# Layer 2's second feed-forward projection as 7 block products on one Trainium2 core

## The reference, cut to what matters

```
mod = silu(c) @ W_mod + b_mod
sh_msa, sc_msa, g_msa, sh_mlp, sc_mlp, g_mlp = split(mod, 6)        # one row of each per sequence
x = x + g_msa * attention(modulate(layernorm(x), sh_msa, sc_msa))
x = x + g_mlp * (gelu(modulate(layernorm(x), sh_mlp, sc_mlp) @ W1 + b1) @ W2 + b2)
```

## Time and profile before

| | |
|---|---|
| median of 3 runs | 2615.79 us (2615.1 to 2616.05) |
| the profiled execution | 2611.51 us, of which the span is 2609.7 us |
| PE busy | 2472.3 us, 95% of the span |
| DVE, ACT, POOL busy | 1777.8, 1208.8 and 546.5 us |
| layer 2's feed-forward part on PE | 1819.0 to 2040.8 us |
| layer 3's attention, then its feed-forward part | to about 2324 us, then to the end |

### The profile page before, as it was taken

One profiled execution on the slowest core, in us unless ns is written; L12 is line 12 of the kernel. 1 busy time (PEld: TensorE's weight loads), 2 busy tenths in 40 slices (PEclk: granted clock), 3 DMA queues, 4 the chain that ended last, 5 costly groups with the idle time before them and its releaser, 6 DMA issues.

```text
span 2609.7 us, 63484 instructions
## 1 busy us (share of the span) xinstructions
PE 2472.3 (95%) x25325; PEld 1913.4 (73%) x25325; DVE 1777.8 (68%) x3912; ACT 1208.8 (46%) x2525; POOL 546.5 (21%) x530
## 2 busy tenths in 40 slices
PE   7998999999999956999999999999999899889999
PEld 6886566666666645888788888887666677679898
DVE  6888788878888675553555555555655598877666
ACT  6886565556555512433333323333434577633333
POOL 2233110001100014663211111111010455500000
PEclk9999999999999967999999999999999999999999
DMA  6000000000000033543400000000000133300000
GB/s 223 3 3 6 25 24 24 24 27 29 24 24 24 20 107 94 137 114 73 135 12 16 16 14 14 16 16 10 0 1 1 58 111 109 94 9 9 17 17 17
DMA packets 77367, 110.82 MB, mean 42 GB/s; under 512 B 11920, under 2 KB 51344, under 8 KB 76688
## 3 DMA queue, kind: packets, MB, share of 16 engines
q1 hardware_dynamic: 71056, 99.99, 12.0%
q0 software_dynamic: 6144, 8.56, 1.8%
HBM read 75.59 MB, written 32.93 MB: 42 GB/s over the span
## 4 chain that ended last, share of the span: by engine, by line
PE 42%; DMA 6%; DVE 3%; SPq 1%; issue 1%; ACT 1%; POOL 0%; DVEq 0%; ACTq 0%
PE psW L351 9%; PE psP L1640 6%; DMA rotated<-work 5%; PE psW L358 4%; PE psS L1832 4%; PE psP L476 4%; PE psO L1640 3%; PE psS L1792 2%; PE psW L1640 2%; PE psO L450 1%; PE psS L417 1%; PE psO L1792 1%; PE psP L433 1%; PE psW L583 1%; SPq L2872 0%
## 5 line engine op out<-in xcount | busy, mean ns | idle before, releaser
L358 PE MATMUL psW<-r,work 128*128 128x512 f32 x1024 | 479.6, 601 | 0.1
L1453 POOL TENSOR_TENSOR work<-work 128x512 f32<-128x512 f32 x128 | 132.2, 1044 | 1046.6 <-DVE work L929 1046.5
L358 PEld LDWEIGHTS psW<-r,work 128*128 128x128 f32 x1024 | 179.7, 190 | 159.8 <-issue 154.5
L351 PE MATMUL psW<-work,r 128*128 128x128 f32 x2048 | 237.9, 277 | 1.9 <-DVE work L895 1.0
L351 PEld LDWEIGHTS psW<-work,r 128*128 128x128 f32 x2048 | 231.4, 192 | 4.7 <-DVE work L1066 1.3
L1353 ACT ACTIVATE work<-work 128x512 f32<-128x512 f32 x128 | 80.1, 626 | 273.8 <-DVE work L908 273.8
L893 DVE TENSOR_TENSOR work<-psW,tab 128x256 f32<-128x256 f32 x64 | 26.9, 420 | 182.3 <-PE psW L344 182.3
L583 PE MATMUL psW<-work,r 128*128 128x128 f32 x1024 | 132.5, 283 | 5.8 <-ACT work L1243 5.8
L2186 ACT ACTIVATE work<-psP 128x512 f32<-128x512 f32 x64 | 38.2, 597 | 209.0 <-PE psP L1640 209.0
L1640 PE MATMUL psP<-r 128*128 128x256 f32 x512 | 127.0, 386 | 5.0 <-DVE r L1925 3.0
L583 PEld LDWEIGHTS psW<-work,r 128*128 128x128 f32 x1024 | 121.0, 194 | 12.8 <-ACT work L1243 4.2
(11 more groups left out here) (371 smaller groups left out, 5540.9 us busy)
## 6 DMA issues: line engine op xcount, KB each, us to landing
r<-in_l_fc SPq DMA_DIRECT2D x16, 1024.0 KB, 6.6
rotated<-work SPq DMA_DIRECT2D x60, 256.0 KB
work<-mod_rows SPq DMA_DIRECT2D x64, 128.0 KB, 2.8
work<-gate_rows SPq DMA_DIRECT2D x64, 128.0 KB, 2.8
work<-rotated SPq DMA_DIRECT2D x30, 256.0 KB
r<-in_l_w SPq DMA_DIRECT2D x2, 3072.0 KB, 14.5
x<-in_x SPq DMA_DIRECT2D x8, 512.0 KB, 10.0
gather_table<-work SPq DMA_DIRECT2D x32, 128.0 KB, 1.8
```

What stands on the lines that cost most here:

```text
L351: ins = nc.tensor.matmul(ps[:, q * P:(q + 1) * P], w[:, k, lo + q * P:lo + (q + 1) * P], L.hT[:, k, :], start=(k == 0), stop=(k == KC - 1))
L358: ins = nc.tensor.matmul(ps[:, 0:width], L.hT[:, k, :], w[:, k, lo:lo + width], start=(k == 0), stop=(k == KC - 1))
L1453: nc.gpsimd.tensor_tensor(E, E, halves(L.rs)[i].unsqueeze(2).broadcast_to([P, 8, N]), ALU.mult).then_inc(L.s[f"prob{i}"].sem, 1)
```

## The change

Layer 2's second half becomes `second`, as in layer 3. `result` for "l2", `back` and `yT` go. Sums of W2's blocks are made by POOL in layer 2's attention, behind tile 1. Since tokens are now on the partitions, gate and b2 have to be there as rows: beside the rows that layer 2's attention uses, the route stage writes the gate and gate x b2 of the feed-forward part to DRAM (1 DVE operation, 4 transposes, 1 copy on ACT, 1 DMA more, and a wait for it ahead of the first expert's modulation). In each group SP loads, each row on 64 partitions, 2 DMAs of 256 KB with gates (L2896 of the new kernel) and 4 of 128 KB with gate x b2 (L2903). POOL adds the latter to x in two operations of 128 x 512 (`pool_l2_bias`). DVE multiplies y by the gates (`f_gated`) and in the next step adds y to x. SP's loads for group n wait until group n-1 is gated. POOL's `pool_rms` now waits for group 6 to be gated, and stands behind the bias operations of all 8 groups.

DVE's moments move from the first half's end to the second half, ahead of `y12`. PE's second turn of the next input moves ahead of F_(1). In the last group DVE waits for `root` 12 three operations later, and ACT begins layer 3's first modulations between its copies.

```diff
--- before.py
+++ after.py
...
-        gate_rows = nc.dram_tensor("gate_rows", [B, 2 * D], FP32, kind="Internal").ap()
+        gate_rows = nc.dram_tensor("gate_rows", [B, 4 * D], FP32, kind="Internal").ap()
...
                 values(0, 2)
-                pe.wait_ge(su["mask4"], 1)
+                after(pe, *Q["l2"].summed(NG - 1, "y11", 0))
+                bias_product()
+                after(pe, *Q["l2"].summed(NG - 1, "y12", 0))
                 rotate(0)
-                bias_product()
...
+        def act_l3_head(a, reached):
+
+            modulate, _, _, biased = act_narrow_parts(a, L[3])
+            if reached == "hidden":
+                modulate(0, 0)
+            if reached == "q2":
+                modulate(1, 0)
+            if reached == "q3":
+                biased(0)
...
                 if L.li == 2 and is_first(t):
                     g.wait_ge(ld["l2"], 64)
                     pool_weight_sums(g, Q["l2"], 0, 0)
+                if L.li == 2 and t == 1:
+                    pool_second_sums(g, Q["l2"], 0, 0)
...
+        def pool_l2_bias(g, n):
+
+            s = Q["l2"].s
+            after(g, s["f_xn"], n + 1)
+            after(g, s["f_in1"], (n + 1) * 64)
+            for h in range(2):
+                xs = x[:, 4 * n + 2 * h:4 * n + 2 * h + 2, :]
+                nc.gpsimd.tensor_tensor(xs, xs, Q["l2"].bias[h], ALU.add).then_inc(s["f_xb"].sem, 1)
...
                 F_(0)
                 G(0)
+                if early and Q.kind == "l2":
+                    after(pe, *Q.summed(t, "c11", M - 1))
+                    turn(t + 1, 1)
                 F_(1)
                 G(1)
-                if early:
+                if early and Q.kind == "moe":
                     after(pe, *Q.summed(t, "c11", M - 1))
                     turn(t + 1, 1)
                 if Q.kind == "l2" and not ahead:
                     pe_l3_head(pe, 0)
 
-            def back(t):
-
-                after(pe, Q.s["f_yt"], t + 1)
-                for r in range(4):
-                    for k in range(KC):
-                        ins = nc.tensor.transpose(psS[:, r * D + k * P:r * D + (k + 1) * P],
-                                                  Q.yT[:, k, r * P:(r + 1) * P], ident)
-                ins.then_inc(Q.s["f_bk"].sem, 1)
...
                 low, high = Q.hid[:, 0:4, :], Q.hid[:, 4:8, :]
+                rotary_next = Q.kind == "l2" and t == NG - 1
+                if Q.kind == "l2" and t == 0:
+                    following(pe, "l2")
                 for m in range(2):
                     if m == 0:
-                        after(pe, *Q.summed(t, "left", 1))
+                        after(pe, *(Q.part(t, "h11", 1) if Q.kind == "l2" else Q.summed(t, "left", 1)))
                     after(pe, *Q.part(t - 1, "y21", m))
                     part(bank_a[m], low, P * m, b11)
-                after(pe, *Q.summed(t, "left", 3))
+                after(pe, *(Q.part(t, "h21", 1) if Q.kind == "l2" else Q.summed(t, "left", 3)))
                 for m in range(2):
                     part(bank_c[m], high, P * m, b21)
                 after(pe, Q.s["f_sum"], 8)
                 for m in range(2):
                     after(pe, *Q.part(t, "q1", m))
                     part(bank_a[m], s2, P * m, t2, False)
+                if rotary_next:
+                    pe_l3_head(pe, 1)
                 after(pe, *Q.summed(t, "s3", 0))
...
-                if Q.kind == "l2":
-                    if t == 0:
-                        following(pe, "l2")
-                    for q in range(KC):
-                        for n, j in enumerate(chunks(t, (0, 1))):
-                            ins = nc.tensor.matmul(psS[:, q * 512:(q + 1) * 512], Q.w2[u][:, j, q * P:(q + 1) * P],
-                                                   Q.hid[:, j, :], start=(n == 0), stop=(n == FJ - 1))
-                        if q == 0 and t == NG - 1:
-                            pe_l3_head(pe, 1)
-                    ins.then_inc(Q.s["f_y"].sem, 1)
-                    return
...
+                if Q.kind == "l2":
+                    after(v, *Q.part(t, "h12", 1))
...
                 after(v, *Q.part(t, "y21", 1))
                 after(v, *Q.summed(t, "y12", 1))
+                if Q.kind == "l2":
+                    after(v, Q.s["f_in0"], (t + 1) * 32)
+                    nc.vector.tensor_tensor(Q.y, Q.y, Q.gate, ALU.mult).then_inc(Q.s["f_gated"].sem, 1)
+                    return
...
+                if Q.kind == "l2" and t == 0:
+                    dve_rsqrt(ch, rstd[:, NT - 4:NT], moments[:, NT - 4:NT, 1])
+                elif Q.kind == "l2":
+                    measure(t - 1)
+                if Q.kind == "l2" and not ahead:
+                    dve_norm(v, ch, L[3], 2)
                 block(t, "y12", 0)
                 block(t, "y12", 1)
                 finish(t, u)
 
             def add(t):
 
-                after(v, Q.s["f_bk"], t + 1)
+                after(v, Q.s["f_gated"], t + 1)
+                after(v, Q.s["f_xb"], 2 * (t + 1))
                 xs = x[:, bass.ds(t * 4, 4), :]
...
-                if Q.kind == "l2":
-                    for q in range(KC):
-
-                        gate = table("gate2f")[:, q, bass.ds(t * 8, 8)].unsqueeze(2).broadcast_to([P, 8, N])
-                        yT = Q.yT[:, q, :]
-                        ch.link(nc.vector.tensor_scalar(yT, psS[:, q * 512:(q + 1) * 512], c("l2_b2", q), None, ALU.add))
-                        y3 = yT.rearrange("p (b n) -> p b n", n=N)
-                        ins = nc.vector.tensor_tensor(y3, y3, gate, ALU.mult)
-                        if q == 0:
-                            ch.link(ins)
-                    ins.then_inc(Q.s["f_yt"].sem, 1)
...
                     norm(t + 1, (t + 1) % 2)
                 if Q.kind == "l2" and t > 0:
                     add(t - 1)
+                c22(t, 0)
+                c22(t, 1)
+                c11(t, 1)
                 if Q.kind == "l2" and not ahead:
                     v.wait_ge(su["root"], 12)
                     dve_norm(v, ch, L[3], 0)
-                c22(t, 0)
-                c22(t, 1)
-                c11(t, 1)
                 c12(t, 0)
                 c12(t, 1)
-                if Q.kind == "l2" and t > 0:
-                    measure(t - 1)
-                if Q.kind == "l2" and not ahead:
-                    dve_norm(v, ch, L[3], 1)
-                if Q.kind == "l2" and t == 0:
-                    dve_rsqrt(ch, rstd[:, NT - 4:NT], moments[:, NT - 4:NT, 1])
+                if Q.kind == "l2":
+                    first_sum(t)
+                    if ahead:
+                        modulate(t + 1, 0)
+                    else:
+                        dve_norm(v, ch, L[3], 1)
...
                 if t >= Q.seconds:
                     return
+                if Q.kind == "l2" and t == NG - 1:
+                    act_l3_head(a, "hidden")
                 after(a, s["f_done"], t)
                 for name, product, r, lo in (("q1", "b", 0, 0), ("q2", "d", 0, P), ("q3", "e", 2, P), ("y21", "g", 2, 0)):
                     for m in range(2):
                         after(a, *Q.product(t, product, m))
                         nc.scalar.activation(Q.y[:, r + m, lo:lo + P], psS[:, 512 * m:512 * m + P], ACT.Copy
                                              ).then_inc(s["f_part"].sem, 1)
+                    if Q.kind == "l2" and t == NG - 1:
+                        act_l3_head(a, name)
...
                 hid(t, u, 0, 1)
                 hid(t, u, 1, 2)
                 hid(t, u, 1, 1)
+                second(t)
...
+                    ch.link(nc.vector.tensor_tensor(mod[:, 6:8, :], table("gate2"), over_batches(c("l2_bout", 0, 2)),
+                                                    ALU.mult))
+                if i == 12:
+                    nc.vector.tensor_tensor(mod[:, 8:10, :], table("gate2f"), over_batches(c("l2_b2", 0, 2)), ALU.mult
                                             ).then_inc(su["mask4"], 1)
...
             pe.wait_ge(su["mask4"], 2)
-            for i, source in enumerate((table("gate2"), mod[:, 6:8, :])):
+            for i, source in enumerate((table("gate2"), mod[:, 6:8, :], table("gate2f"), mod[:, 8:10, :])):
...
             a.wait_ge(su["turned_rows"], 2)
-            nc.scalar.activation(rows0, psS[0:B, 512:512 + 2 * D], ACT.Copy).then_inc(su["rows"], 1)
+            rows_ff = Q["moe"].gT[0:B, 0, :]
+            nc.scalar.activation(rows0, psS[0:B, 512:512 + 2 * D], ACT.Copy)
+            nc.scalar.activation(rows_ff, psS[0:B, 0:2 * D], ACT.Copy).then_inc(su["rows"], 1)
...
+            after(sp, L[2].s["xupd"], NT)
+            s2 = Q["l2"].s
+            for n in range(NG):
+                after(sp, s2["f_gated"], n)
+                for b in range(2):
+                    sp.dma_start(Q["l2"].gate[b * N:(b + 1) * N],
+                                 gate_pairs[b:b + 1, 4 * n:4 * n + 4, 2 * D:3 * D].broadcast_to([N, 4, D])
```

(20 more changed lines are left out.)

90 lines of the change are left out of this document (48 added, 42 removed).

## The result

The changed kernel takes 2618.24 us (median of 20 runs, 2611.47 to 2623.97) where the kernel before, run beside it, takes 2613.82 (20 runs, 2608.7 to 2618.28). The ratio is 1.002 with an interval of 1.0014 to 1.0026. The prediction was 2608.8, with a range up to 2613: a gain of 7.0 us was forecast and a loss of 4.4 measured. Both the sign and the range were wrong.

The account below looks back on a forecast made before the run. PE was taken to bound layer 2's feed-forward part, busy all 27.58 us of a step. Terms of -16.9, +3.0, +4.9, +1.7 and +0.3 gave -7.0, from 2615.8 to 2608.8 us, range 2600 to 2613.

Parts of the forecast that it names:

- narrow form for wide, turns back gone: Layer 2's feed-forward second half on PE: each step falls from 27.58 to 25.47 us, -16.9 over 8 groups.
- POOL beside DVE: Groups 1 to 5: DVE operations on SBUF wait out POOL's, making s1 late for PE; +3.0 us, between 1 and 7.
- stop at layer 3's first tile: Last group: PE waits for POOL's rms, held behind the last bias pair, and DVE's norm; +4.9 us.
- clock after it: After PE's stop at layer 3's first tile, records run at the lower 1.2 GHz level; +1.7 us (0 to 1.8).
- The +0.3 of the route stage: Route stage: a small DVE operation and 4 transposes more, +0.3 us (0 to 1).
- Rival 3: PE's narrow matmuls are bound by weight loads, 16.1 us more a step: 2745 us; chance 0.01.
- the landing of the bias rows, H + 8.8: Each group's last bias DMA lands 3.4 us after its start, 8.8 us after H, the group's first product's start.
- mild form of rival 2: Milder POOL-DVE lock loss, around 1 to 1.5 us a group, ending between -2 and +2: 2616 us; chance 0.09.
- rival 2: Late bias rows make the POOL-DVE lock bite in every group, 3.4 us each: net +17, 2633 us; chance 0.07 in full.
- Rival 1: Last group: the chain to the rms is short or hidden, or the clock does not fall: 2601.5 us; chance 0.24.
- rival 4: The change does not do what it says and layer 2's wide path remains: 2616 us; chance 0.01.
- A stop in every group: Layer 2's feed-forward groups: PE stopping in each one was listed as a sign of the prediction being wrong; no size given.

Follow-up runs that it names:

- e5: Changed kernel with bias-row DMAs before the gate's wait, weight sums first, rms before the last bias pair, pairs tied to the previous group's x + y: 2597.42 us.
- e1: Changed kernel with POOL's rms for layer 3 placed ahead of the last bias pair instead of behind it: 2610.84 us.
- e6: Changed kernel with the bias rows' four DMAs issued ahead of the gate's two, both still behind the wait for gating: 2607.65 us.
- e2: Changed kernel with POOL's weight sums placed ahead of the bias pairs instead of behind them: 2610.85 us.
- e7: Changed kernel with POOL's bias pair cut to 8 of 256 columns, the rest of the bias left out: 2609.51 us.

## Why the prediction was wrong, point by point

| term of the sum | forecast | measured in the stage |
|---|---|---|
| narrow form for wide, turns back gone | -16.9 | -16.5 |
| POOL beside DVE | +3.0 | +10.4 |
| stop at layer 3's first tile | +4.9 | +7.1 |
| clock after it | +1.7 | +2.8 |
| sum | -7.3 | +3.8 |

The +0.3 of the route stage lies ahead of the stage and makes the -7.0 of the forecast.

**The narrow form was right.** Groups 0 and 6 show it in the changed kernel, groups 1 to 5 in e5 and the last in e1: 26.69 (1819.02 to 1845.71 in the trace of before) to 25.47 in the first, which had no turns back to lose; 27.58 to 25.47 in five and to 25.52 in group 6; 29.59 to 26.92 in the last. That is 1.22 + 5 x 2.11 + 2.06 + 2.67. The weight loads do not bind at 128 columns in fp32: rows of 16 records start 1.78 apart, as in layer 3, so that one takes a quarter of the 0.429 of a record with 512 columns. Rival 3 is refuted. The ratio of 0.62 by the Trainium skill's "TensorE: Matmul & The Clock Gate", section "Back-to-back issue gap", does not hold here; these rows give 0.26.

**The step that failed is the landing of the bias rows, H + 8.8.** They came at H + 11.3 in the last group (11.6 in group 1, 10.4 in group 4), and two terms were worked out from that time. Gating was at H + 2.7, as forecast (2.8). Of the 2.5 us, 0.6 are the issue, 0.61 each in place of 0.52 for six DMAs, and 1.8 are the landing, 5.2 in place of 3.4. I had taken 3.4 from rows of before in which a load of 128 KB had SyncE's queue to itself, with "since a megabyte is under way" as the only allowance for 512 KB ahead of it. e6 puts this right on one point, the order of the DMAs, and gets a stage within 1.2 us of the forecast.

**What it did to POOL beside DVE (+3.0, came to +10.4).** In groups 1 to 4 the prediction has the pair run to H + 11.3, beside PSUM work, and the sum alone hold `first_sum`, for about the slack of 0.9. Both the slack (0.9) and the wait for a whole POOL operation came out. With the pair about 2.5 us later it holds `first_sum` and the sum holds the modulation or s1 (groups 1 to 3); with the pair 1.6 later (group 4) the sum starts just ahead of `first_sum` and holds it for 2.1. 1.84, 1.43, 1.76 and 1.47 in place of 0.25 each, and 3.87 in place of 2.0 in group 5, where the four sums of 1.27 meet L2010 to L2015. e6, with the pair 0.1 to 0.7 later than forecast, loses 0 to 0.6 in groups 1 to 4, so the forecast would have been about right at its own landing time.

The prediction held this case as the mild form of rival 2, "around 1 to 1.5 a group, ends between -2 and +2", at 0.09, and rival 2 turned on rows landing "3 us or more later than I take, near H + 12". The mechanism and the place were on paper, the threshold was not: 1.6 us later already cost 1.5 in group 4. The result of +4.4 lies above the mild form's +2 too, since stop and clock cost more than their terms. The chance was too small, because the landing lay within the spread of the rows it rested on (2.6 to 7.2).

**The last group** had the right chain, POOL from the bias pair through the rms to L344, and the right cure of it is e1. The stop was 2.2 longer than forecast, by the same late landing. The clock cost 2.8 and not 1.7, a size of its own: PE stayed at the lower level for two rows of records, not one. With stops of 7.3, 5.4 and 5.1 (e2, e6, e7) it cost 1.5, 2.6 and 2.1, so it does not follow the stop's length in these four.

**The numbers beside the sum.** In group 5 three operations at 1.07 less 0.9 make 2.3 and not the 2.0 taken. And the rivals that end above 2613 (rival 2 in both forms, 3 and 4) have 0.18 together, where the prediction put 0.15 above its range. Neither changes how it came out. The 0.9 of turns back that it left open for the last group are indeed not gained, as told for the stretch behind the stage.

**Rival 1** (a short chain) did not occur, and rival 4 neither. What the prediction gave as signs came out: 25.5 in groups 0 and 6, the narrow half at 12.5, one large stop at L344, the clock after it. "A stop in every group", the sign it gave for being wrong, came out in groups 1 to 5.

**What stays open.** How the landing divides into a fixed time and what is queued around it: e6 moved the order and the start of the loads together. What the lower clock in layer 3's beginning costs in the median, since each kernel has one profile. And the chain told under e2, from the weight sum over DVE's root to the late pair, is read from the traces: no kernel has the weight sum first in each group and keeps it off the root. Where the sum does not stand first (the changed kernel, e1, e7) L757 takes 0.17 and the pair of group 1 starts at H + 11.6 to 11.7.

## What to carry to other kernels

Work given to an engine that is idle nearly 80% of the time is not free if its operands share SBUF with DVE: what decides is which DVE instruction it meets and how much of the POOL operation is still to come then. So ask where in the step it will start, and tie it to an event there (e5) instead of to the arrival of a DMA. Look as well at what it meets in the place that it is moved to: the weight sums of e2 met a tiny operation there, whose delay made the next DMAs late. When one uncertain time enters several terms, as a landing that starts a chain does, move it by its whole spread and add up all terms at once; each looked small here, and together they turned the sign. And in an in-order queue put the piece with a late consumer (the gate) behind the piece with an early one (the bias), and the step that the bound engine waits for (the rms) ahead of one that nobody wants yet.
